# A gated-linear-attention block on one core: where k is turned, weighed and q grown in the order of the steps

## The reference, cut to what matters

```python
def step(s, inp):                      # 8192 tokens, 16 heads of 64
    qi, ki, vi, gi = inp
    s = exp(gi)[:, :, None, None] * s + ki[..., :, None] * vi[..., None, :]
    return s, einsum('bhk,bhkv->bhv', qi, s)

h = layernorm(x) * (1 + ca) + sa
q, k, v = h @ Wq.T, h @ Wk.T, h @ Wv.T
k = k * sigmoid(h @ Wg.T)
g = -softplus(h @ Wd.T + bd)           # log decay, one per head and token
out = scan(step, q, k, v, g)
out = out * rsqrt(mean(out * out) + eps) * norm_w * sigmoid(h @ Wog.T)
x = x + ga * (out @ Wo.T)
h = layernorm(x) * (1 + cb) + sb
x = x + gb * ffn(h)                    # token shift, squared relu, gate
```

## Time and profile before

| what | before |
|---|---|
| time, median of 3 runs (lowest to highest) | 3366.9 us (3357.97 to 3368.17) |
| span of the profiled execution, first to last instruction | 3361.3 us |
| TensorE busy | 3248.8 us, 97% |
| weight loads of TensorE busy | 2997.7 us, 89% |
| VectorE busy | 1878.7 us, 56% |
| ScalarE busy | 1299.4 us, 39% |
| GpSimd busy | 466.3 us, 14% |
| mean granted clock of TensorE | 0.990 of full speed |

### The profile page before, as it was taken

One profiled execution on the slowest core, in us unless ns is written; L12 is line 12 of the kernel. 1 busy time (PEld: TensorE's weight loads), 2 busy tenths in 40 slices (PEclk: granted clock), 3 DMA queues, 4 the chain that ended last, 5 costly groups with the idle time before them and its releaser, 6 DMA issues. The chain is left out here.

```text
span 3361.3 us, 99256 instructions
## 1 busy us (share of the span) xinstructions
PE 3248.8 (97%) x37253; PEld 2997.7 (89%) x37253; DVE 1878.7 (56%) x4825; ACT 1299.4 (39%) x3584; POOL 466.3 (14%) x723
## 2 busy tenths in 40 slices
PE   7999999999999999999999996999999999999998
PEld 6899899899899999999999986998889989998887
DVE  5444444444444444444444445766777677667776
ACT  3444444444444444444444444333333333333332
POOL 0111111111111111011111112211111111111110
PEclk8999999999999999999999998999999999999999
DMA  5221222222322222213222125223322222223320
GB/s 207 68 94 66 78 94 65 91 77 69 96 69 75 94 65 88 83 65 98 70 70 96 63 76 164 82 75 87 87 76 75 75 75 80 82 75 90 85 75 26
DMA packets 273353, 279.30 MB, mean 83 GB/s; under 512 B 24720, under 2 KB 221344, under 8 KB 273072
## 3 DMA queue, kind: packets, MB, share of 16 engines
q1 hardware_dynamic: 270960, 270.67, 26.4%
q10 hardware_dynamic: 2112, 4.19, 0.4%
HBM read 189.84 MB, written 84.93 MB: 82 GB/s over the span
## 5 line engine op out<-in xcount | busy, mean ns | idle before, releaser
L55 PE MATMUL psJ<-h_hi,w_g_hi 128*128 128x256 f32 x1024 | 321.2, 314 | 37.1 <-DVE qg L852 31.6
L55 PE MATMUL psJ<-h_hi,w_q_hi 128*128 128x256 f32 x1024 | 309.1, 302 | 3.1 <-DVE kg L843 3.1
L932 DVE SCALAR_TENSOR_TENSOR mid<-state,w_all,psB 128x64 f32<-128x64 f32 x256 | 71.7, 280 | 428.4 <-PE psB L649 353.6
L55 PE MATMUL psG<-h_hi,w_og_hi 128*128 128x256 f32 x1024 | 287.9, 281 | 8.7 <-PEq L347 4.7
L55 PE MATMUL psJ<-h_hi,w_k_hi 128*128 128x256 f32 x1024 | 288.0, 281 | 0.7 <-ACT w_new L739 0.7
L56 PE MATMUL psJ<-h_lo,w_g_hi 128*128 128x256 f32 x1024 | 286.5, 280 | 0.0
L56 PE MATMUL psJ<-h_lo,w_q_hi 128*128 128x256 f32 x1024 | 286.3, 280 | 0.0
L57 PE MATMUL psJ<-h_hi,w_q_lo 128*128 128x256 f32 x1024 | 286.0, 279 | 0.0
L57 PE MATMUL psJ<-h_hi,w_k_lo 128*128 128x256 f32 x1024 | 285.8, 279 | 0.0
L57 PE MATMUL psJ<-h_hi,w_g_lo 128*128 128x256 f32 x1024 | 285.5, 279 | 0.0
L56 PE MATMUL psJ<-h_lo,w_k_hi 128*128 128x256 f32 x1024 | 285.2, 279 | 0.0
(11 more groups left out here) (238 smaller groups left out, 9505.1 us busy)
## 6 DMA issues: line engine op xcount, KB each, us to landing
cum_rows<-cum_dram SPq DMA_DIRECT2D x512, 64.0 KB, 3.8
grown<-cum_dram SPq DMA_DIRECT2D x256, 128.0 KB
o_dram<-o SPq DMA_DIRECT2D x256, 128.0 KB, 2.3
o_cols<-o_dram SPq DMA_DIRECT2D x128, 256.0 KB, 5.0
an_norm_x<-in_L_attn_x_dram SPq DMA_DIRECT2D x32, 512.0 KB, 6.4
h_dram<-h_hi SPq DMA_DIRECT2D x32, 512.0 KB, 2.8
h_dram<-h_lo SPq DMA_DIRECT2D x32, 512.0 KB, 4.5
h_hi<-h_dram SPq DMA_DIRECT2D x32, 512.0 KB, 3.9
```

Source lines behind the costliest of these rows:

```text
L55: nc.tensor.matmul(out, w_hi, x_hi, start=first, stop=False)
L932: nc.vector.scalar_tensor_tensor(out=into, in0=mid[:, p % 2, m - 1, :] if m else state[:, p, :], scalar=w_all[:, c, b, p:p + 1], in1=psK[: ...
```

## The change

The next pair's k is turned inside this step's last product. In step p < 7 the two transposes of pair p + 1 are issued ahead of the third chunk (k == 2) of this step's k projection (in step 0, of v5; in the last tile, which has no projections, by themselves at the end of the step), behind a wait for this step's `prob`. The turn of the next tile's pair 0 is issued in the tail's k projection. VectorE makes `kw` and `qg` of pair p + 1 at the end of step p, ahead of `rest_h` in step 0 and of `gate_k`, which is now of pair p - 1 in each step; in the tail it makes those of pair 0 between the copies of the decay weights and `gate_k` of pair 7. The layer norm of steps 4 and 5 stands behind `gate_k`.

```diff
--- before.py
+++ after.py
@@ -518,7 +518,7 @@
             sp.wait_ge(s["h_kept"], 32 * NT)
 
 
-        def project(i, kind, b, pe, turns_decay=False, ready=None):
+        def project(i, kind, b, pe, turns_decay=False, ready=None, turned=None):
 
             u = USES.index((kind, b))
             bank = psJ[u % 2]
@@ -528,6 +528,8 @@
                     pe.wait_ge(s["h_lo"], KD * i + k + 1)
                 if ready and k == KD - 1:
                     ready()
+                if turned and k == 2:
+                    turn_k(pe, *turned)
                 if kind == "v":
                     c, at, n = (b // 2, b % 2 * VZ, VZ) if b < 4 else (b - 4, 0, 512)
                     hh, hl = (a[:, k, c * CH:(c + 1) * CH] for a in (h_hi, h_lo))
@@ -541,6 +543,14 @@
                                         t["ident"][:, :]).then_inc(s["n_turned"], 1)
             last.then_inc(s["proj"], 1)
 
+        def turn_k(pe, j, p):
+            n = NP * j + p
+            pe.wait_ge(s["k"], n + 1)
+            hold(pe, s["prob"], n)
+            for c in range(NC):
+                last = nc.tensor.transpose(psX[:, c, :], kg[:, p, c * CH:(c + 1) * CH], t["ident"][:, :])
+            last.then_inc(s["kT"], 1)
+
         def turn_x(pe, n):
             pe.wait_ge(s["xn"], NC * (n + 1))
             hold(pe, s["hT"], KD * n)
@@ -602,12 +612,7 @@
                     finish_mod(pe, MOD_STEPS.index(p - 1))
                 if p == (1 if gla else 4) and prep:
                     turn_x(pe, i + 1)
-                if gla:
-                    pe.wait_ge(s["k"], n + 1)
-                    hold(pe, s["prob"], n)
-                    for c in range(NC):
-                        last = nc.tensor.transpose(psX[:, c, :], kg[:, p, c * CH:(c + 1) * CH], t["ident"][:, :])
-                    last.then_inc(s["kT"], 1)
+                behind = (j, p + 1) if gla and p + 1 < NP else None
                 if p == 6 and proj:
                     pe.wait_ge(s["g_raw"], i + 1)
                     pe.wait_ge(s["hT"], KD * (i + 2 if prep else i + 1))
@@ -656,18 +661,20 @@
                 if not proj and p >= 2:
                     turn_w(pe, p - 2)
                 if p == 0 and gla:
-                    project(j, "v", 5, pe)
+                    project(j, "v", 5, pe, turned=behind)
+                elif behind and not proj:
+                    turn_k(pe, *behind)
                 if p > 0 and proj:
                     project(i, "q", p - 1, pe)
                     if p == 6:
                         pe.wait_ge(s["w_new"], i + 1)
-                    project(i, "k", p - 1, pe, p == 6)
+                    project(i, "k", p - 1, pe, p == 6, turned=behind)
                 if p == 4 and proj:
                     for b in range(4):
                         project(i, "v", b, pe)
             if proj:
                 for kind in KINDS:
-                    project(i, kind, NP - 1, pe)
+                    project(i, kind, NP - 1, pe, turned=(i, 0) if kind == "k" else None)
 
         @block.tensor
         def _(pe):
@@ -853,6 +860,16 @@
                                     q[:, p, :].rearrange("p (c b t) -> p c b t", b=2, c=NC), grown[:, p % 2, :].rearrange(
                 "p (b c t) -> p c b t", b=2, c=NC), ALU.mult).then_inc(s["qg"], 1)
 
+        def weigh_k(dve, j, p):
+            n = NP * j + p
+            dve.wait_ge(s["kT"], n + 1)
+            hold(dve, s["inc"], n)
+            nc.vector.tensor_tensor(
+                kw[:, :, :].rearrange("p c (h d) -> p c h d", h=2),
+                psX.rearrange("p c (h d) -> p c h d", h=2),
+                w_cur[:, 2, :, 2 * p:2 * p + 2].unsqueeze(3).to_broadcast([P, NC, 2, DH]),
+                ALU.mult).then_inc(s["kw"], 1)
+
         def weigh_mod(dve, m):
             dve.wait_ge(m_loaded[m % 2], 16 * (m // 2 + 1))
             hold(dve, s["m_read"], m)
@@ -906,20 +923,9 @@
                     dve.wait_ge(s["zb"], i + 1)
                     nc.vector.scalar_tensor_tensor(out=zt[:, 2, :, :], in0=zt[:, 1, :, :], scalar=-1.0,
                                                    in1=zt[:, 1, :, :], op0=ALU.mult, op1=ALU.min).then_inc(s["softin"], 1)
-                if gla:
-                    if p == 0:
-                        dve.wait_ge(s["cur"], i)
-                    dve.wait_ge(s["kT"], n + 1)
-                    hold(dve, s["inc"], n)
-                    nc.vector.tensor_tensor(
-                        kw[:, :, :].rearrange("p c (h d) -> p c h d", h=2),
-                        psX.rearrange("p c (h d) -> p c h d", h=2),
-                        w_cur[:, 2, :, 2 * p:2 * p + 2].unsqueeze(3).to_broadcast([P, NC, 2, DH]),
-                        ALU.mult).then_inc(s["kw"], 1)
-                if proj and p > 1 and p != 5:
+                if proj and not gla and p > 1 and p != 5:
                     gate_k(dve, i, p - 2)
                 if gla:
-                    grow_q(dve, j, p)
                     if not proj and p >= 3:
                         rest_w(dve, p - 3)
                     dve.wait_ge(s["score"], n + 1)
@@ -937,9 +943,6 @@
                     nc.vector.tensor_tensor(pr, pr, psS, ALU.mult).then_inc(s["prob"], 1)
                 if gla and (p > 0 or not opens):
                     sum_o(dve, n - 1, (p - 1) % NP)
-                if p == 0 and proj:
-                    for k in range(KD):
-                        rest_h(dve, i, k)
                 if p == 5 and proj:
                     dve.wait_ge(s["l"], i + 1)
                     nc.vector.scalar_tensor_tensor(out=zt[:, 0, :, :], in0=zt[:, 1, :, :], scalar=0.0, in1=zt[:, 2, :, :],
@@ -955,17 +958,24 @@
                     dve.wait_ge(s["n_turned"], i + 1)
                     hold(dve, s["n_rows"], 32 * i)
                     nc.vector.tensor_copy(cum_out[:, :], psN).then_inc(s["n_out"], 1)
+                if gla and p + 1 < NP:
+                    weigh_k(dve, j, p + 1)
+                    grow_q(dve, j, p + 1)
+                if p == 0 and proj:
+                    for k in range(KD):
+                        rest_h(dve, i, k)
                 if p == 0 and not gla:
                     norm_stats(dve, i + 1)
                     norm_x(dve, i + 1)
+                if proj and (p > 0 if gla else p == 4):
+                    gate_k(dve, i, p - 1)
                 if p == 4 and prep > 1:
                     norm_stats(dve, i + 2)
                 if p == 5 and prep > 1:
                     norm_x(dve, i + 2)
-                if p == 4 and proj:
-                    gate_k(dve, i, p - 1)
             if proj:
-                gate_k(dve, i, NP - 2)
+                if not gla:
+                    gate_k(dve, i, NP - 2)
                 dve.wait_ge(s["w_new"], i + 1)
                 hold(dve, s["state"], NP * i)
                 for h in range(2):
@@ -973,6 +983,9 @@
                     nc.vector.tensor_copy(w_all[r, :, :, :],
                                           w_new[r, 3:5, :].rearrange("p b (g h c) -> p h c b g", c=NC, h=2)[:, h, :, :, :])
                 nc.vector.tensor_copy(w_cur[:, :, :, :], w_new[:, 0:3, :].rearrange("p a (h c) -> p a c h", c=NC)).then_inc(s["cur"], 1)
+                dve.wait_ge(s["cur"], i + 1)
+                weigh_k(dve, i, 0)
+                grow_q(dve, i, 0)
                 gate_k(dve, i, NP - 1)
 
         @block.vector
```

## The result

| | before | after |
|---|---|---|
| time, median of 4 runs (lowest to highest) | 3366.4 us (3357.97 to 3368.17) | 3318.55 us (3317.58 to 3322.23) |
| span of the profiled execution | 3361.3 us | 3315.6 us |
| ratio of the times, 95% interval | | 0.9868 [0.9856, 0.9881] |

The forecast was 3319 us. The change saves 47.9 us, 1.3%. The span fell by 45.7 us, and 42.6 of them are in the 31 full tiles: from one tile's `psC` products (the running sums of the decay, in step 6) to the next tile's, the distances add up to 1902.1 us before and 1859.5 after. That is 1.37 us per tile.

A forecast was written before the change was run, and what follows sets the result against it. TensorE, busy for 97% of the span, was taken to bound the kernel. 60.6 us of stops removed, less 10.5 and 2 us added, gave 48 us off the 3366.9 us median: 3319 us, range 3303 to 3347.

The forecast's parts named there:

- The releaser: Before g's last chunk (L55): this step's kw, started 0.89 to 0.95 us earlier, ends the stops; rival of another releaser 0.05.
- So every one of the stops should go, the `h_lo` and the v3 wait included: Before g's last chunk: kw made a step earlier, 1.97 us available against 1.38 needed, removes all stops, 60.6 us.
- (a): The 61 long stops before g's last chunk, steps 1 and 5, removed: 31.6 + 61 x 0.23 = 45.6 us.
- (b): The short stops before g's last chunk in steps 2, 3, 4 and 7 removed: 0.12 us on average, 15 us.
- (c): Each turn waits for this step's prob inside a product: 0.12 us per tile in v5, 2 us in step 6.
- (d): Step 0: the turn puts off v5's end and the chain to g by 0.22 us; with (c) there 10.5 us.
- A wait in the middle of a product: At the turns: an already fulfilled wait inside an accumulating product taken to cost nothing; at most 26 us.
- The rival of 3345 us: Waits inside the products cost a reload, 0.12 us at each of seven turns, 26 us off the gain; chance 0.12.
- The load of grown: For qg of pair 0 in the tail: 3.3 us to land in the median, 7.5 at most; landing by 1028.8 costs nothing.
- the rival's chain: Late grown delays qg of pair 0, kg of pair 7, then v5; 31 us per further 1 us late; chance 0.03.

The follow-up runs named there:

- qg_late: The kernel before, with the multiplication qg moved on VectorE from ahead of the states to behind prob: 3368.89 us, ratio 1.0021.
- tensor_only: TensorE's part of the change alone, turns inside the products, with VectorE's queue in the order of the kernel before: 3356.92 us, ratio 0.9988.
- logits_behind: The kernel before, with VectorE's wait for v3's logits and two operations behind it moved behind kw and qg of step 5: 3346.97 us, ratio 0.9957.
- ready_first: The changed kernel, with the nine waits of ready() in step 1 ahead of g's first chunk instead of its last: 3309.08 us, ratio 0.9841.
- waits_twice: The changed kernel, with the nine waits of ready() in step 1 issued twice in a row at the old place: 3330.66 us, ratio 0.9898.
- turn_at_second: The changed kernel, with each turn ahead of the second chunk instead of the third: 3347.07 us, ratio 0.995.
- kw_last: ready_first with pair 1's turn behind v5, its qg behind h_lo, and the wait for kw last of the nine: 3295.93 us, ratio 0.9792.
- the half on VectorE alone: VectorE's new order with TensorE turning k as before: 3468.27 us, ratio 1.0315; with step 4's norm statistics moved ahead of kw, 3379.99 us.
- grown_last: The changed kernel, with SyncE's two grown loads in step 7 issued behind the spread loads of pairs 0 to 3: 3416.95 us, ratio 1.0164.

## Why the prediction was right, and the step that failed

The total was right: 48 us forecast, 47.9 measured. It was right in part by two errors against each other.

**The releaser, right and shown.** The stops ended with `kw`, not with the `qg` that the view of waits names. qg_late moved `qg` and no stop moved with it; tensor_only left `kw` in its place and the long stops stayed; logits_behind took away what `kw` of step 5 stood behind, and that stop became a short one.

**"So every one of the stops should go, the `h_lo` and the v3 wait included": the step that failed.** For step 5 and the short stops it held. In step 1 the distance fell from 0.74 to 0.50 us in the median, not to 0.12. The last `h_lo` is written at 1011.56, and the product that should have started at 1011.77 started at 1012.22. The prediction asked when each thing would be there and gave the waits themselves no price, on the ground that nine fulfilled ones cost nothing in step 6. In step 1 the queue is held until the last `h_lo` and then has eight of the nine waits ahead of the next weight load. In step 6 nothing holds it: its four wait instructions stand at 1009.76 to 1010.08 in the trace of the kernel before, 0.7 us ahead of the product at 1010.78, while products ahead of it are still to run. ready_first shows the cost by taking the waits from behind `h_lo`, waits_twice by doubling them. In the term (a) the mean distance fell from 0.79 to 0.48 us and the start behind it stayed at 0.19, so 0.31 us were won in step 1 instead of 0.69; v5 took another 0.06 more than forecast. The stretch of step 1 ended 0.41 per tile above its forecast, 13 us in all. What brought the total back was not foreseen: steps 2 to 4 and 7 gave 0.66 us per tile where the terms (b) and (c) have 0.41, 8 us; step 0's stretch another 0.07, 2 us; and 3 us of the span's difference lie outside the full tiles. Of these 2.6 lie ahead of the first `psC` products, whose start varies from 84.6 to 88.8 us over the traces of this study: chance, not the change.

**The short stops, undersized.** The 0.12 on average counted as (b) was 0.15 to 0.18 in steps 2 to 4. The stops themselves, by start distances, were 0.05 and 0.08 in the start behind, 0.13 together. Part of the rest is likely the pace described below; that is argued, not shown.

**`prob` in step 6, (c).** Counted at 2 us and not there: step 7's stretch, in which that k lies, fell by 0.15.

**The turn in v5, (c) and (d), right.** v5 lasts 3.26 instead of 2.86 us, 0.40 where 0.34 was forecast, and g is still 1.43 behind it in most tiles (1.56 to 1.75 in six). Of the 0.40, 0.12 is the wait for `prob`; that it goes by how late `prob` is there is shown by turn_at_second. The rest is the turn itself. It could be avoided: kw_last has the turn behind v5, hidden under the wait for `h_lo`, once the waits ahead of g stand in the right order.

**A wait in the middle of a product: nothing**, as taken. The rival of 3345 us wanted 0.12 us more at each turn, and the turn has the same 0.46 us inside k after the change, at either chunk, as it had between two products before.

**The load of grown** lands in time for TensorE, as forecast. The 3.3 us taken for it were the median of all transfers of that tensor; where `qg` of pair 0 waits for the load, it starts 4.6 to 5.0 us behind its issue. In 12 of the full tiles that wait is 0.18 to 0.99 us (before, once), and v5's first product still comes 0.15 us behind the one before it in every tile, as before the change: the slack took it. Once the load is late the rival's chain runs as described, and dearer than its 31 us for each us, since the clock falls too.

## What to carry to other kernels

When a stop on the busiest engine ends, price two things: what was waited for last, and the wait instructions that still stand behind that one in the queue. Put a group of waits so that the one that is fulfilled last is the last of the group, and put the group where the queue is ahead of its engine; here that took the ratio from 0.9868 to 0.9792, with one turn moved back. And when an engine's work is moved forward, look at what stands behind it there in its worst step: of the 107 us that the half on VectorE alone cost, 88 came through the statistics of one layer norm. And a profile that names one releaser for a wait on several semaphores can be wrong: move the named instruction, and see whether the stop moves.

## What the hardware showed that was not expected

- **Fulfilled waits have a price once the queue is held.** 0.106 us for each wait instruction. In the passes that are written out, outside TensorE's loop, the same place in the kernel after has a distance of 0.12 us, although the last `h_lo` is as late (its four subtractions end at 111.37); inside the loop it is 0.46 to 0.60. The trace shows another order there, not another price: the wait for the last `h_lo` stands on the weight load itself, and the four wait instructions stand ahead of it, at 111.09 to 111.41, while earlier products run. Where waits_twice has too many to fit there they cost 0.106 us each in the written-out tile too, and the distance is 0.44. So the same lines of source can get either order. In the first tile:

```profile
111.53 0.28 PE L57 MATMUL psJ<-h_hi,w_g_lo 128*128 128x256 f32 x1
111.65 0.28 PE L55 MATMUL psJ<-h_hi,w_g_hi 128*128 128x256 f32 x1
```

- **Two paces of the same product.** Undisturbed products of 256 columns follow each other after some 0.113 or some 0.118 us, at the same granted clock, and mostly keep one or the other over many products until a break. The mean over the tiles was 0.1155 us before, 0.1151 after, 0.1149 in ready_first and 0.1159 in qg_late. With some 9,000 such products in the pass, 0.0004 us is some 4 us. What sets the pace stays open.
- **The clock fell with 2.79 us of idle time** in grown_last and stayed at half for the six products of v5 ahead of the turn, 2.7 us. The same is to be seen without that change: in six of the 31 tiles, before and after alike, TensorE stands for 1.7 to 2.8 us at the start of step 0 with nothing to wait for that the profile shows (13.9 us before, at most 12.3 us after, under `issue`). They are every fourth tile, each the first of a new turn of TensorE's loop of four tiles. After two of the six in each kernel some seven products of v4 come 0.43 us apart, as from 1124.12 in the kernel after (a stop of 2.19 us) and from 657.53 in the one before (2.84). The length of the stop alone does not decide it: before, the clock fell after 2.19 us in one tile and held after 2.38 in another.
